# Buffers moved to 64-byte starts, and the weight split moved from chunk 7 to chunk 4 of a slot

## The reference

```
xn = layernorm(x)                              # no gain, no bias
s  = causal_attention(xn) @ w_out              # 16 heads of 16, softmax over 1024 keys
y  = xn
for i in range(6):                             # six blocks, 256 -> 1024 -> 256
    y = gelu(y @ W1[i].T + B1[i]) @ W2[i].T + B2[i] + y
    if i < 5: y = layernorm(y) * LN_G[i] + LN_B[i]
out = x + s * silu(y)
```

## Time and profile before

| | us |
|---|---|
| median of three runs | 1671.97 |
| lowest, highest | 1671.54, 1676.83 |
| the profiled execution, its own time | 1672.36 |
| its span | 1670.7 |
| TensorE matmuls busy | 1617.1 (97%) |
| VectorE busy | 1169.8 (70%) |
| ScalarE busy | 856.2 (51%) |
| GpSimd busy | 317.8 (19%) |
| mean granted clock of TensorE | 0.992 |

### The profile page before, as it was taken

One profiled execution on the slowest core, in us unless ns is written; L12 is line 12 of the kernel. 1 busy time (PEld: TensorE's weight loads), 2 busy tenths in 40 slices (PEclk: granted clock), 3 DMA queues, 4 the chain that ended last, 5 costly groups with the idle time before them and its releaser, 6 DMA issues. The chain is left out here.

```text
span 1670.7 us, 28636 instructions
## 1 busy us (share of the span) xinstructions
PE 1617.1 (97%) x11024; PEld 1314.5 (79%) x11024; DVE 1169.8 (70%) x2932; ACT 856.2 (51%) x1164; POOL 317.8 (19%) x305
## 2 busy tenths in 40 slices
PE   6989999999999999999999999999999899999998
PEld 5879988889888888888888888888989844444443
DVE  7826777777777777777777677776565568787753
ACT  3444444444443444444444444444444499798986
POOL 1021111111111111111111111111011123343333
PEclk9989999999999999999999999999999989999999
DMA  8868724536002002012030020022020135565341
GB/s 276 320 173 209 174 62 109 116 73 140 15 7 61 8 16 49 7 34 42 7 51 8 23 51 9 14 39 80 1 71 1 45 114 163 162 187 178 117 116 58
DMA packets 76017, 141.46 MB, mean 85 GB/s; under 512 B 10172, under 2 KB 52924, under 8 KB 68540
## 3 DMA queue, kind: packets, MB, share of 16 engines
q1 hardware_dynamic: 75880, 139.62, 32.0%
HBM read 109.44 MB, written 55.31 MB: 99 GB/s over the span
## 5 line engine op out<-in xcount | busy, mean ns | idle before, releaser
L646 ACT ACTIVATE m_hid<-m_h_ps,m_b1s 128x512 f32<-128x512 f32 x384 | 265.3, 691 | 694.1 <-PE m_h_ps L749 674.6
L712 DVE TENSOR_TENSOR m_hidl<-m_hid,m_hidh 128x512 fp32r<-128x512 f32 x384 | 283.1, 737 | 266.5 <-ACT m_hidh L649 265.6
L993 ACT ACTIVATE a_prob<-a_st_ps 128x1024 f32<-128x1024 f32 x288 | 277.6, 1023 | 40.4 <-PE a_st_ps L1079 36.9
L762 PE MATMUL m_y_ps<-shared,m_hidh 128*128 128x256 f32 x1536 | 283.1, 282 | 0.0
L749 PE MATMUL m_h_ps<-m_xth,shared 128*128 128x512 f32 x768 | 275.7, 400 | 6.3 <-issue 3.9
L613 POOL TENSOR_TENSOR xres<-xres,m_b2s 128x1024 f32<-128x1024 f32 x48 | 132.1, 2753 | 744.1 <-DVE xres L665 744.1
L649 ACT ACTIVATE m_hidh<-m_h_ps,m_b1s 128x512 fp32r<-128x512 f32 x384 | 261.7, 682 | 0.0
L762 PEld LDWEIGHTS m_y_ps<-shared,m_hidh 128*128 128x128 f32 x1536 | 246.8, 188 | 14.5
L762 PE MATMUL m_y_ps<-w2h,m_hidh 128*128 128x256 f32 x768 | 216.9, 282 | 0.0
L762 PE MATMUL m_y_ps<-shared,m_hidl 128*128 128x256 f32 x768 | 215.3, 280 | 0.0
L762 PE MATMUL m_y_ps<-w2l,m_hidh 128*128 128x256 f32 x768 | 214.2, 279 | 0.0
(11 more groups left out here) (121 smaller groups left out, 2656.6 us busy)
## 6 DMA issues: line engine op xcount, KB each, us to landing
shared<-k_stacks SPq DMA_DIRECT2D x14, 896.0 KB
shared<-q_stacks SPq DMA_DIRECT2D x14, 896.0 KB
q_stacks<-q_parts SPq DMA_DIRECT2D x96, 128.0 KB
k_stacks<-k_parts SPq DMA_DIRECT2D x96, 128.0 KB
q_parts<-mq SPq DMA_DIRECT2D x16, 512.0 KB, 4.3
k_parts<-mk SPq DMA_DIRECT2D x16, 512.0 KB, 3.8
mk<-k_stacks SPq DMA_DIRECT2D x20, 384.0 KB, 10.7
raw<-w1t SPq DMA_DIRECT2D x48, 128.0 KB, 2.3
```

The source lines that it names most:

```text
L646: nc.scalar.activation(hid[n % 2][:], h_ps[n % 2][:], ACT.Gelu, bias=b1s[i % 2][:, k:k + 1])
L712: nc.vector.tensor_tensor(hidl[n % 4][:], hid[n % 2][:], hidh[n % 4][:].bitcast(F32), ALU.subtract).then_inc(low_done, 1)
L762: m = nc.tensor.matmul(y_ps[:, j, :], h[n % 4][:, j * P:(j + 1) * P], w[par][:, k, :], start=(k == 0 and j % 2 == 0 and h is hidh and w is ...
L993: nc.scalar.activation(to, scores, ACT.Exp).then_inc(exp_done, 1)
```

## The change

1. `mhalf`, the tile of 4 columns that holds -0.5, is allocated first, with 16 columns (64 bytes) of which the first 4 are used. Behind it comes `x_mx0`, one of the two tiles for the maxima (256 bytes), which stood behind `x_unused`. The same operations read and write them. From then on every operand of TensorE starts at a multiple of 64 bytes: `shared`, `apart` and `ident` move up by 320 bytes, `mq`, `mk`, `va` and `xres` by 288, the `w1h` group, `m_xth`, `m_xtl`, `m_hidh` and `m_hidl` by 32. So the distance between `shared` and what it is multiplied with changes by 288 bytes, and the distance between the `w1h` group and what it is multiplied with stays as it was.
2. VectorE splits the weight piece at chunk 4 of the slot in place of chunk 7: behind low(4) and the variance, ahead of the visit of chunk 4.

```diff
--- before.py
+++ after.py
@@ -135,13 +135,13 @@
 class MaxSearch:
 
 
-    def __init__(s, nc, b, scratch, keep):
+    def __init__(s, nc, b, scratch, keep, mx):
         s.nc, s.scratch = nc, scratch
         s.q, s.k = stack_views(keep["mq"]), stack_views(keep["mk"])
         s.apart = None
         s.causal, s.ident = keep["causal"], keep["ident"]
         s.unused = b.sb("x_unused", [P, 2, 2, BANK], BF16)
-        s.mx = [b.sb(f"x_mx{u}", [P, 2, HG, QT]) for u in range(2)]
+        s.mx = [*mx, b.sb("x_mx1", [P, 2, HG, QT])]
         s.nm = b.sb("x_nm", [P, PARTS, HG * QT])
         s.nmt = b.sb("x_nmt", [PARTS * HG * QT, P])
         s.loaded = [b.sem(f"x_loaded{u}") for u in range(2)]
@@ -342,7 +342,7 @@
         @block.gpsimd
         def _(pool):
             nc.gpsimd.memset(ident[:], 0.0).then_inc(ident_ready, 1)
-            nc.gpsimd.memset(keep["mhalf"][:], -0.5).then_inc(half_ready, 1)
+            nc.gpsimd.memset(keep["mhalf"], -0.5).then_inc(half_ready, 1)
             nc.gpsimd.memset(keep["causal"][:], 0.0).then_inc(half_ready, 1)
             nc.gpsimd.memset(keep["ones"][:], 1.0)
             pool.wait_ge(ident_ready, 1)
@@ -356,7 +356,7 @@
                 nc.gpsimd.memset(keep["va"][u][:, :, :, HD:2 * HD], 1.0)
             for g in range(GROUPS):
                 pool.wait_ge(var_ready, g + 1)
-                nc.gpsimd.tensor_tensor(rstd[g % 2][:], var[g % 2][:], keep["mhalf"][:], ALU.pow).then_inc(rstd_ready, 1)
+                nc.gpsimd.tensor_tensor(rstd[g % 2][:], var[g % 2][:], keep["mhalf"], ALU.pow).then_inc(rstd_ready, 1)
 
         @block.vector
         def _(dve):
@@ -613,7 +613,7 @@
                 nc.gpsimd.tensor_tensor(xx, xx, b2s[i % 2][:].broadcast_to([P, TILES, DIM]), ALU.add).then_inc(b2_added, 1)
                 if t < NORMED:
                     pool.wait_ge(var_ready, t + 1)
-                    nc.gpsimd.tensor_tensor(rstd[:], var[:], keep["mhalf"][:], ALU.pow).then_inc(rstd_ready, 1)
+                    nc.gpsimd.tensor_tensor(rstd[:], var[:], keep["mhalf"], ALU.pow).then_inc(rstd_ready, 1)
             for n in range(2):
                 augment(nc, pool, keep, n)
 
@@ -714,7 +714,7 @@
                     low_x(t + 1)
                 if t:
                     epilogue(t - 1, k)
-                if k == 7 and t < LAST:
+                if k == 4 and t < LAST:
                     dve.wait_ge(raw_loaded[g % 2], 32 * (t // 2 + 1))
                     split_piece(nc, dve, keep, (i + 1) % 2, g, w_high, t + 1).then_inc(w_split, 1)
                 for v in AT.get(n, ()):
@@ -1147,10 +1147,12 @@
     }
     with ExitStack() as ctx:
         b = Bufs(nc, ctx)
+        mhalf = b.sb("mhalf", [P, 2 * PARTS * TILES])[:, 0:TILES]
+        mx = [b.sb("x_mx0", [P, 2, HG, QT])]
         apart = [b.sb(f"apart{u}", [P, PAIR * SEQ], F32R) for u in range(2)]
         shared = [b.sb(f"shared{n}", [P, HALVES * HID], F32R) for n in range(4)]
         keep = {
-            "ident": b.sb("ident", [P, P]), "mhalf": b.sb("mhalf", [P, TILES]), "causal": b.sb("causal", [P, BANK]),
+            "ident": b.sb("ident", [P, P]), "mhalf": mhalf, "causal": b.sb("causal", [P, BANK]),
             "ones": b.sb("ones", [SPARE, 1, P]),
 
 
@@ -1165,7 +1167,7 @@
             "part_stored": [[b.sem(f"part_stored{u}{m}") for m in range(4)] for u in range(2)],
 
         }
-        search = MaxSearch(nc, b, scratch, keep)
+        search = MaxSearch(nc, b, scratch, keep, mx)
         with ExitStack() as inner:
             b = Bufs(nc, inner)
             keep |= {
```

## The result

The changed kernel took 1663.12 us (median of four runs, 1662.35 to 1664.12) against 1672.84 for the kernel before, timed beside it (four runs, 1671.54 to 1676.83): a ratio of 0.9938, 95% interval 0.992 to 0.9957. The forecast was 1683, slower; what came is nearest to the first rival (1666), in which GpSimd does not hold VectorE up. The profiled execution took 1664.12 us, 8.2 less than the one before.

What follows compares the result with a forecast made beforehand. TensorE was taken as the bound, busy nearly all the time in the blocks. Terms -12.1 + 10.2 + 15.7 - 3.0 = +10.8 us on 1672.4 gave 1683; range 1660 to 1691, the forecast's own 1677 to 1690.

Steps and rivals of the forecast that it cites:

- the first rival: At chunk 4 GpSimd does not hold VectorE up; visits cost 1 us, buffers give 5.4; time 1666, chance 0.28.
- waits at the boundaries: At the five block boundaries `up` no longer waits 2.07 us each for VectorE's split of the last weight piece: -10.4 us.
- clock at 920 us: At one block boundary TensorE no longer runs 3.4 us at 1.2 GHz from 920.2, after its pause: -1.7 us.
- first slot, wait and clock: In the first slot TensorE waits 7.7 us for the late first weight piece, then 2.5 us for a slower clock: +10.2 us.
- VectorE at chunk 4: At chunk 4 the split meets GpSimd's power operation, which holds VectorE up and delays TensorE: +15.7 us, bounds 1 and 21.
- buffers: `shared` blocks take the faster matmul pace of the `w1h` group through the new distances: -3 us, bounds -11.5 and 0.
- I take 0.8, near the upper end: Hold-up of VectorE's split by GpSimd's power operation at chunk 4: 0.8 us a slot, bounds 0 and 1.02.
- The prediction's own sign: In slots 3 to 39 the split's span becomes 2.1 us; the prediction is wrong if it stays 1.3.
- The room at chunk 4: VectorE's idle time after chunk 4, 1.39 us in 21 slots, less 0.1 as TensorE needs the visit sooner; 1.29 us fits.
- the prediction's rule: In 21 slots with visits at chunks 4 and 5, TensorE loses VectorE's lateness less 0.15 us, one for one.
- rival 4: Starts at multiples of 64 slow every matmul: `w1h` blocks take the pace of `shared`, +5 us; 1691, or 1674 without hold-up; chance 0.07.
- Rivals 3 and 4: Starts at multiples of 64 make every matmul faster (3: about 1650, chance 0.09) or slower (4: 1691, chance 0.07).

Runs made afterwards that it cites:

- buffers only: The changed kernel with its new buffer placing kept but the split put back at chunk 7: 1664.86 us, ratio 0.9952.
- the addition of 320 columns: The changed kernel plus an unused GpSimd addition of 320 columns between the variance and the power operation: 1668.11 us, ratio 0.997.
- the filler: The changed kernel plus an unused VectorE statistics operation at chunk 4: 1666.89 us between variance and split, 1666.64 us behind the split.

## Why the prediction was wrong

| term | foretold | measured | from |
|---|---|---|---|
| waits at the boundaries | -10.4 | -10.6 | buffers only to after |
| clock at 920 us | -1.7 | -1.6 | the same, slot 32 |
| first slot, wait and clock | +10.2 | +11.0 | buffers only to after, slots 0 and 1 |
| VectorE at chunk 4 | +15.7 | -1.0 | buffers only to after, ordinary slots |
| buffers | -3.0 | -6.6 | before to buffers only |
| sum | +10.8 | -8.9 (before rounding) | |

The two profiled spans differ by 8.3 us: 8.9 less in the slots and 0.6 more outside them. Of the 19.7 us between the two sums, 16.7 are in one row.

**The step that failed** is "I take 0.8, near the upper end, because the nearest row shows a wait up to the other's end". The bounds (0 and 1.02) held the truth, and it lay at the lower one. The row taken was line 239 beside an addition of 1024 columns in 2.78 us. What that row and the power operation have in common is the pair of engines; what they don't is the number of columns and the kind of operation. The addition moves 1024 columns in 2.78 us, about 2.7 ns a column; the power operation moves 4 and takes 1.02 us all the same, so by an estimate from the addition's pace (0.01 us for 4 columns) next to none of its time is moving data, and the row of before already said so. The prediction's own sign came: the split's span stayed at 1.3 us. What the runs showed in its place: where GpSimd went first, VectorE's second copy was held 0.02 us by the power operation on 4 columns, 0.55 us by the addition of 320 columns (0.72 us long), and past the end by a memset of 2048. The bound "0 if it holds the ports only for its 4 columns" was the right number, with the first rival's price. That the columns decide fits all of these, but no run varied the columns of one kind of operation: that it is the columns and not the kind is argued, not shown.

The Trainium skill (SBUF — State Buffer, "Who interferes with whom") says that the engine that issues first keeps the pair of ports for its whole instruction. The memsets agree with it (copies of 1.71 and 1.98 us in place of 0.29), and so does the addition of 320 columns in both orders; the power operation does not: with 1.02 us under way it held the copy 0.02. The prediction put line 239 under that section's copies and two-input operations; it is neither, but an operation on one tile and a constant.

**The rest of that term was sound.** The room at chunk 4 (1.39 - 0.1 us) took the bare split of 1.29 us, and lateness beyond it costs about what was reckoned: the prediction's rule gives 21 x (0.41 - 0.15) = 5.5 us for the 0.41 us that the addition cost VectorE (the split's span went from 1.29 to 1.70 us in the mean), and 21 x (0.34 - 0.15) = 4 for the filler's 0.34 (the copy's start behind it); the slot sums rose by 4.5 and 2.3, the timed runs by 5 and 3.5. By the same rule a hold-up of 0.8 us would have come out near the forecast; no run had one that long. Two sums of the prediction are off by a little: by its own counts a hold-up of 1.02 us is 0.87 x 21 + 0.52 x 7 = 22 us, not 20 or 21, and rival 4 without the hold-up is 1676, not 1674.

**The first slot** came out to 0.1 us in its times, and its price to less than 1 (11.0 us in the two slots, 10.6 by the run with the first three at 7): a queue's order that can be read in the trace of before is safe ground.

**The buffers** brought what the first rival had (5.4) and a little more: 4.4 us over 18 ordinary `shared` slots is 0.24 a slot, where the earlier trace rows gave 0.19. Of the 10.4 us that the chunk's 54 ns (6 x 3.6 + 12 x 2.7) would make over 192 chunks, 6.6 came out; that the rest is work of VectorE that does not get shorter is argued, not shown. The guess of -3 halved an effect whose cause, the distance, had been named as a possibility; its further guess, that VectorE takes part of it back at chunk 5, was already in the rows that it started from. The Trainium skill (TensorE: Matmul & The Clock Gate, "Step-by-step: what each phase is for") says that loading the next weights takes no read bandwidth from the running matmul. The prediction read from it that no placing would matter, and these runs, in which 32 bytes of padding cost 15 us, speak against that; they don't show whether it is the loading that is slowed. Rivals 3 and 4, on the start at 64, both fell: the pace of the `w1h` blocks stayed (230.5 and 230.8 ns), and all starts at 32 above a multiple of 64 gave the same paces as all at 64.

## What to carry to other kernels

- An engine's duration is not the time for which it occupies what it shares. Before a row of contention is carried over to another instruction, compare the columns moved and the operation, not only the engines; and look at single slots, since a mean can mix two orders.
- Moving work earlier moves its needs earlier: look up the first iteration by itself, where the transfer has no lead. Here the first three of 40 splits cost 10.6 us, as much as all five block boundaries gave, and one condition in the code gave it back.
- Where TensorE is the bound, try the placing of its operands against each other in steps of 32 bytes: it costs some unused bytes and no instruction, and here the best and the worst of three distances lay 1% apart.

## What the hardware showed that was not expected

- The pace of float32 matmuls depends on the distance between weights and partners in a partition: of the three tried, 64 modulo 128 gives 230.8 and 115.6 ns (512 and 256 columns), 32 modulo 64 gives 234.4 and 118.4, 0 modulo 128 gives 232.6 and 119.2. Starts at 0 or 32 modulo 64 make no difference when the distance is kept. The distance of a matmul's own two operands is not all: 32 bytes ahead of `m_hid` took `up` to 232.0 ns.
- The power operation of GpSimd on 4 columns takes 1.02 us alone. Started just before VectorE's second copy, it took 1.19 us in 34 of 37 slots, where the copy went first; in the 3 where it went first itself it held the copy 0.02 us. An addition of 320 columns in the same place held it 0.55.
